# Two 64-byte gaps around the split weights of a graph network layer

## The reference

```python
h = jnp.maximum(_layernorm(x, axis=-1), 0.0)
agg = segment_sum(edge_features, dst) / max(counts, 1)
combined = jnp.concatenate([agg, h], axis=1)      # (50000, 320)
h1 = jax.nn.relu(combined @ W1 + b1)              # (50000, 512)
out = x + h1 @ W2 + b2                            # (50000, 256)
```

## Time and profile before

| | us |
|---|---|
| median of 3 runs | 1351.27 |
| lowest, highest | 1351.22, 1351.97 |
| the profiled execution | 1351.55 |
| its span, first to last instruction | 1350.0 |
| TensorE busy | 1325.3 (98%) |
| DVE busy | 1209.5 (90%) |
| ACT busy | 695.8 (52%) |
| POOL busy | 542.3 (40%) |

### The profile page before, as it was taken

The page is one execution under the profiler, slowest core; times in us unless marked ns, Lnnn a source line. Parts: engine busy times, 40 slices in busy tenths (PEclk is TensorE's granted clock), DMA queues, the critical chain, the costliest instruction groups (busy, mean ns, idle before and its releaser), DMA issues.

```text
span 1350.0 us, 29143 instructions
## 1 busy us (share of the span) xinstructions
PE 1325.3 (98%) x6968; PEld 1119.1 (83%) x6968; DVE 1209.5 (90%) x3059; ACT 695.8 (52%) x1281; POOL 542.3 (40%) x710
## 2 busy tenths in 40 slices
PE   4999999999999999999999999999999999999999
PEld 2788888888888888888888888888888888888887
DVE  5898999899999999999999999999999899989997
ACT  3554545454545454545454545454545455555553
POOL 6434343434343434343434343434343434343431
PEclk9999999999999999999999999999999999999999
DMA  4455454545454545454545454545454555555542
GB/s 112 107 135 133 120 134 119 136 118 138 116 142 111 143 111 147 109 144 109 144 111 142 113 141 113 141 115 139 116 137 117 137 118 135 119 134 121 132 110 77
DMA packets 422724, 168.59 MB, mean 125 GB/s; under 512 B 321188, under 2 KB 422326, under 8 KB 422712
## 3 DMA queue, kind: packets, MB, share of 16 engines
q1 hardware_dynamic: 421720, 167.28, 50.7%
q10 hardware_dynamic: 992, 1.18, 0.3%
HBM read 66.12 MB, written 51.40 MB: 87 GB/s over the span
## 4 chain that ended last, share of the span: by engine, by line
PE 95%; SPq 2%; POOL 1%; DMA 1%; issue 1%; DVE 1%; ACT 0%; POOLq 0%; DVEq 0%
PE P L920 26%; PE P L922 13%; PE P L897 13%; PE P L899 13%; PE P L898 13%; PE P L906 6%; PE P L907 6%; PE PA L886 1%; PE PA L885 1%; DMA dst_w<-in_dst_dram 0%; SPq L313 0%; PE PA L881 0%; SPq L301 0%; SPq L314 0%; SPq L275 0%
## 5 line engine op out<-in xcount | busy, mean ns | idle before, releaser
L920 PE MATMUL P<-w_both,H_hi 128*128 128x512 f32 x1564 | 557.6, 398 | 0.5 <-DVE H_lo L725 0.5
L603 ACT ACTIVATE H_hi<-P 128x512 fp32r<-128x512 f32 x392 | 233.6, 596 | 503.6 <-PE P L907 503.6
L922 PE MATMUL P<-w_both,H_lo 128*128 128x256 f32 x1564 | 440.6, 282 | 0.0
L920 PEld LDWEIGHTS P<-w_both,H_hi 128*128 128x128 f32 x1564 | 295.0, 189 | 72.5 <-DVE H_lo L725 1.0
L725 DVE SCALAR_TENSOR_TENSOR H_lo<-P,H_hi 128x512 fp32r<-128x512 f32 x392 | 266.4, 680 | 82.6 <-ACT H_hi L603 79.6
L897 PE MATMUL P<-HT_hi,w_hi 128*128 128x512 f32 (+1 forms) x784 | 312.8, 399 | 1.9 <-ACT w_both L617 1.9
L899 PE MATMUL P<-HT_hi,w_lo 128*128 128x512 f32 (+1 forms) x784 | 308.5, 393 | 0.0
L898 PE MATMUL P<-HT_lo,w_hi 128*128 128x512 f32 (+1 forms) x784 | 306.2, 391 | 0.0
L443 POOL TENSOR_TENSOR XB<-X,b_row 128x1024 f32<-128x1024 f32 x98 | 237.8, 2427 | 169.0 <-DVE O L739 165.7
L922 PEld LDWEIGHTS P<-w_both,H_lo 128*128 128x128 f32 x1564 | 294.0, 188 | 3.8
L437 POOL TENSOR_TENSOR E_both<-ES,E_both 128x256 fp32r<-128x256 f32 x98 | 73.0, 745 | 401.2 <-ACT E_both L583 401.2
(11 more groups left out here) (77 smaller groups left out, 1157.7 us busy)
## 6 DMA issues: line engine op xcount, KB each, us to landing
HQ<-HN SPq DMA_DIRECT2D x388, 128.0 KB, 3.2
out_dram<-O SPq DMA_DIRECT2D x97, 512.0 KB, 3.3
X<-in_x_dram SPq DMA_DIRECT2D x96, 512.0 KB, 3.4
ER<-in_edge_attr_dram SPq DMA_DIRECT2D x392, 32.0 KB, 1.7
DT<-table_dram SPq DMA_DIRECT2D x392, 1.0 KB, 1.7
X<-in_x_dram ACTq DMA_DIRECT2D x1, 512.0 KB, 5.5
w_raw<-in_L_gnn_W_dram ACTq DMA_DIRECT2D x4, 128.0 KB, 5.2
w_raw<-in_L_gnn_W_dram SPq DMA_DIRECT2D x2, 256.0 KB, 3.9
```

The lines of the kernel that those rows point to most:

```text
L603: act.activation(H1_hi[:, m, nodes(t)], bank(m)[:, nodes(t)], ACT.Relu).then_inc(s_1hi, 1)
L920: pe.matmul(out_bank(j)[some, :], H1_hi[:, m, rows], w2_both[:, m, :, :].rearrange("p a d -> p (a d)"), start=(m == 0), stop=False)
L922: last = pe.matmul(out_bank(j)[some, 0:D], H1_lo[:, m, rows], w2_both[:, m, 0, :], start=False, stop=(m == CH - 1))
```

## The change

Two small tensors are declared that nothing reads or writes:

```diff
         w2_raw = sb("w2_raw", [P, CH, D])
+        beside_w = sb("beside_w", [P, 16])
         w1_hi = sb("w1_hi", [P, CD, H], F32R)
...
         w2_both = sb("w2_both", [P, CH, 2, D], F32R)
+        beside_x = sb("beside_x", [P, 16])
```

## The result

| | before | after |
|---|---|---|
| median, lowest to highest, us (5 runs each) | 1351.53, 1351.22 to 1351.97 | 1365.90, 1364.28 to 1367.65 |
| ratio to before, 95% interval | | 1.0105, 1.0094 to 1.0116 |
| profiled execution, span | 1351.55, 1350.0 | 1364.42, 1362.8 |

The change costs 14.4 us, 1.05%. No change was forecast, and the time lies above the range. Lines of the kernel after are two higher: L899 is L897 of before, L922 is L920, L277 is L275.

A forecast was written before the change was run, and what follows sets the result against it. TensorE was taken to bound the kernel through the distance between matmul starts. Weights, activations and DMA summed as 0 + 0 + 0, leaving a forecast of 1351.3 us, range 1342 to 1356.

The forecast's parts named there:

- What bounds the kernel: TensorE in the loop: number of matmuls times the distance between their starts, 13.44 us a tile, 98 tiles 1317 us.
- I take 0 there as well: First layer's stationary operand, the weights moved 64 bytes on: gain taken as 0.
- The excess of 15.3 ns: First-layer matmul's time above one column per cycle at full clock; all that an address could cost there.
- the 33.1 of a pair: Second-layer pair's excess in ns above one column per cycle at full clock, 353.1 against 320.
- Comparisons 1 and 2: Aligned edge matmuls pay an excess too, 7 ns; second-layer pairs take 5.1 to 9.9 ns more than first-layer rates give.
- Comparison 3: Last group, 80 nodes: pairs take 343.3 ns with w2_both's offset unchanged, so the extra follows the stationary operand's width.
- The moving operand's offset: Rival, second layer: the offset costs 5.1 to 9.9 ns a pair; faster, 1343.3 or 1335.8 us; chance 0.17.
- The two operands come into step: Rival, every matmul: reads at the same place hinder each other; 45.9 us slower, 1397.2 us; chance 0.10.
- Its tenth of the price: A tenth of the in-step rival's price over all matmuls: 4.6 us, giving 1355.9 us.
- DMA, "I take 0": X, O, HN, HQ moved 128 past a multiple of 256: cost 0, since moves half as long again land in time.
- the cover of 1.8: us between the fourth move's landing at 698.3 and DVE's read of HQ at 700.06, in one loop tile.
- The rival of late moves: Moves twice as long make TensorE wait 0.84 us a tile: 82 us, 1433.6; chance 0.04, shared with a slower DVE.

The follow-up runs named there:

- e5: Kernel before with weights and TensorE's other operands both 64 bytes on, DMA tensors unmoved against 256: 1351.3 us, ratio 0.9999.
- e6: Kernel before with weights unmoved and TensorE's other operands moved to 64 past a multiple of 256, distance 0: 1349.1 us, ratio 0.9986.
- e1: Kernel before with the weights alone 64 bytes on, nothing else moved against 256, distance 0: 1348.9 us, ratio 0.9983.
- e4: Kernel before with only the tensors that DMAs touch 128 bytes on, against 256: 1357.0 us, ratio 1.0048.
- e8: Kernel before with only HN, HQ, ER and DT 128 past a multiple of 256: 1356.6 us, ratio 1.0040.
- e15: Kernel before with only HQ, which the moves write, 128 past a multiple of 256: 1358.3 us, ratio 1.0052.
- e14: Kernel before with only HN, which the moves read, 128 past a multiple of 256: 1351.8 us, ratio 1.0002.

## Why the prediction was wrong

- **What bounds the kernel**: right. All of the steady loss is in the distance between the starts of matmuls, and 9.0 of 14.4 us are 97 tiles times 0.093.
- **"I take 0 there as well"** for the weights: wrong, and this is the step that failed. It asked whether a tensor's own offset costs, and no single offset does: e5 and e6 put the operands at other places and get back the values of the kernel before and of e1. What counts is the distance of two operands, and the change took it from 192 to 128. That made a first-layer matmul 4.0 ns longer, 229.0 to 233.0, where the sum had 0. The reason given for this 0 was that the loads from `H1_hi` and `H1_lo`, at a multiple of 128, are not cheaper; but those stood at the second layer's slowest distance, so they could not show it. The excess of 15.3 ns should read 228.8 - 213.3 = 15.5; nothing hangs on it. Of it and of the 33.1 of a pair, the distance moves 5.7 and 6.2 ns on the mean, and nothing in the trace of before shows two distances on one shape.
- **Comparisons 1 and 2** were tilted by the effect that they should find. The line went through 228.8 ns, a value of distance 192. Through the settled 226.7 and 153.3 it has 0.417 ns per column, one column per cycle; it gives 120.0 at 256 columns and 346.7 for a pair, which is the fastest pair measured (346.9). So the pair's 353.1 held an address effect of 6.2 ns.
- **Comparison 3** misled. The narrow pair is cheaper at distance 192 (three take 1.036 us to the nanosecond, 345.3 ns each and not 343.3), and I read this as "the load, and not the address". But in e1, at distance 0, three of the same narrow pairs take 1343.98 - 1342.92 = 1.06 us, 353.0 ns each, no less than 352.5 with 128 columns. The gain by width comes and goes with the distance, so width and address act together.
- **The moving operand's offset** (faster): the change gave 2.0 ns a pair, 3.1 us, less than its lower price, and took 4.0 ns a matmul in the first layer, which this rival left at its old value.
- **"The two operands come into step"** (slower): the right sign and nearly the right place, a pair of operands that hinder each other, with 4.0 of its 11.2 ns in the first layer. Its rule was wrong: distance 0, fully in step, is the first layer's fastest (e1), and after the change the operands were not in step against 256. Its tenth of the price, 4.6 us, was half of what TensorE lost, 9.0, and the range ended there.
- **DMA, "I take 0"**: wrong by 5.7 us (e4, with 2.3 to either side), though the size of the delay was foreseen. A move lands 1.0 us later, inside the cover of 1.8, and the usual tile stays at 13.447. But that cover was read in one tile in the middle of the loop. At the end, and in part at the start, the chain runs through SP and the DMAs, 2% and 1% of it, and there a later landing is paid; and in e4 and e8 some tiles of the loop were late too. The rival of late moves asked for 2.4 us more per move, because it too looked at a steady tile only. Nor did it reckon with the clock, which fell behind the longest wait of the kernel after and cost 1.7 us there.
- The Trainium skill (DMA: Bandwidth & Descriptors, How a descriptor splits into AXI transactions) says that a transaction must start at a multiple of 256 bytes; worked out from that, an estimate, a piece of 256 bytes at 128 past one takes 12 beats instead of 8. For the side written the runs agree in kind: the share of q1 goes from 50.7% to 68.6% in e15. For the side read, which is what its rule speaks of, e14 shows no cost at all (48.5%).
- The Trainium skill (SBUF — State Buffer, Who interferes with whom) says that the next weights' load and the running matmul have ports of their own. The excess here depends all the same on the distance between weights and moving operand, by up to 5.7 ns a matmul (227.8 to 233.5).
- The forecast of rows: DVE and ACT kept their durations (680 ns before and after for `H1_lo`), as said. A difference of over 0.6 ns between matmuls was named as what would make it wrong, and that came.

Still open is why these distances: whether the running matmul's reads meet the load of the next weights or something else of the same matmul was not tried apart, and no law behind 0 and 192 on one side and the six others on the other was found. Open is also what the 13.4 ns are that every matmul pays at full clock. What the traces add is that both are absent at half clock, and that the effect of the distance changes with the width of the stationary operand (80 or 128) and the columns of the moving one (336 or 512). That the effect repeats every 256 bytes rests on e4, e5 and e6, which moved groups by 256 or more and kept their values to 0.1 ns.

## What to carry to other kernels

Where TensorE sets the time of a loop and its matmuls stand further apart than one column per cycle, try the distance in SBUF between stationary and moving operand, in steps of 32 bytes and for each kind of matmul by itself; here that was worth 10 us of 1351 and a "rounder" alignment cost 9. Move one group at a time and bring everything behind it back to its old place, or the gap moves a second thing: here it moved the target of a DMA. And read the cover of a transfer at the start and the end of a program too, where no work has been done ahead.

## What the runs showed that was not expected

- Spacing of float32r matmuls depends on the distance of their operands against 256 bytes: 227.8 to 233.5 ns for 512 columns, 346.9 to 353.1 ns for a pair of 512 and 256, not smoothly, at a granted clock of 0.99 to 1.00.
- At a granted clock of 0.50 the same matmuls take 426 to 428 ns at every distance; at full clock 13.4 ns above one column per cycle are left at the best distance, for 512 columns as for 336.
- 256-byte pieces written to SBUF 128 bytes past a multiple of 256 raise the DMA engines' share from 50.7% to 68.6% and the landing from 3.2 to 4.2 us; read from there they cost nothing (48.5%, 3.1 us). The 1024-byte rows of loads and stores don't mind (50.8%).
- Behind an idle stretch of 2.22 us TensorE ran 3.4 us at half clock in the kernel after, so a late transfer can cost more than the wait (here 1.7 us more).
- In the loop of the kernel before a tile repeats to 1 or 2 ns, so a single profiled execution resolves effects of 0.1 ns a matmul that medians of whole runs, which scatter by 0.2%, would need many runs to see.
